# Gated retention block: totals of o's squares taken as rows by one product with a constant, and o scaled by a row in SBUF

## The chip, the core and the metric

The kernel runs on one core of a Trainium2 chip. The core has TensorE (PE, matrix products into PSUM), VectorE (DVE), ScalarE (ACT), GpSimd (POOL, which can't read PSUM) and the DMA queue of SyncE (SP). They run side by side and wait for each other by semaphores. The metric is the device time of one execution in microseconds. An f32 product stands as two records in the trace.

## What is computed

From the reference, cut to what matters. xn is the layer norm of x; T is 128 tokens, 8 chunks to each of 4 sequences, so 32 chunks.

```python
h = rmsnorm(xn, qkv_norm_w);  q, k, v = h @ quant(qkv_w).T
# per chunk of 128 tokens, 16 heads of 64:
o   = scale * (masked(q k^T) v  +  decay * q S);   S = lam_T * S + k_decayed^T v
out = o * rsqrt(mean(o*o) + 1e-6) * norm_w                     # first norm
out = out * rsqrt(mean(out*out) + 2**-23) * proj_norm_w        # second norm
s   = out @ quant(proj_w).T
g   = silu(xn @ ternary(ffn_w).T + bias)
result = x + s * g
```

Both norms of o together are one factor for each token, worked out from two totals over the 1024 channels: A = mean(o*o) and B = mean((o*norm_w)**2). The factor is (F32_EPS * (A + NORM_EPS) + B) ** -0.5.

## The kernel before

An iteration i takes two chunks, c = 0 and 1; there are NB = 16 iterations, and chunk number g = 2i + c. Channels lie on the partitions, so o of a chunk is 8 tiles of 128 channels by 128 tokens (ow, o_hi, o_lo). The order on each engine is written out by hand in tensor_program, vector_program, scalar_program and gpsimd_program, and nothing is moved by a scheduler.

The path of one chunk from its outputs to its projection:

- DVE weight_o (L1406) takes o out of PSUM with its channel weights into ow; ACT square_o makes the squares sq.
- POOL sum_squares (L2182, L2186, L2191) folds the squares over the 8 tiles into sq_sum[:, c], two planes of 128 channels by 128 tokens, one for A and one for B.
- PE output_scale (L857) multiplies each plane, as the stationary operand, by the column mean_w: two columns of totals, tokens on the partitions. For the three chunks of summed_at_once, (0,0), (1,0) and (15,1), it takes the totals from sq itself (L851) instead.
- DVE output_scale (L1429, L1431) makes F32_EPS * (A + NORM_EPS) + B, one column og.
- POOL output_scale (L2197) raises the column to the power -0.5, then (L2201) puts it on the diagonal diag of the identity.
- PE spread_gamma (L868) multiplies diag by the constant matrix mean_sq, which puts the factors as a row on all partitions, in PSUM.
- DVE scale_o (L1415) multiplies ow by that row; ACT high_o (L1898) and DVE split_o (L1422) split it into o_hi and o_lo.
- PE project_out (L880) waits for o_lo.

In the steady iterations (i >= 3) PE does the totals of chunk (i, 0) between the ffn products p7 and p3 (L680), its spread after p4, then the outputs of (i, 1) (L830, L834), update_state (L811), and both halves of project_out(i, 0). The totals of chunk (i, 1) come in the next iteration, between project_qk 1 and 2 (L747), the spread between 2 and 3, and project_out(i, 1) after project_qk 3 and k_product p1. On DVE low_b_sum (L1222) stands between output_scale and scale_o there, on chunk (i, 0) it is the gate work take_z12 and take_z21 (L1285).

Of the kernel before, what the change touches and what calls it, by code (L numbers as in the profile page):

```python
# [5 lines left out]
ALU = mybir.AluOpType  # L6
# [7 lines left out]
P = 128  # L14
BANK = 512
T = 128
CHUNKS = 2
# [19 lines left out]
def program(nc, x, qkv_w, proj_w, decay, ffn_w, ffn_b, norm_cols, x_turned, out):  # L37
# [17 lines left out]
    with ExitStack() as ctx:  # L55
# [92 lines left out]
        norm_pair = sb("norm_pair", [P, 2, CHUNKS, 2])  # L148
        og = sb("og", [P, 2, 4])
        diag = sb("diag", [P, CHUNKS, T])  # L150
        sum_cols = sb("sum_cols", [P, PR, 2])
# [309 lines left out]
        for i in range(BY_TOKENS):  # L461
            if i > 0:
                for j in range(PR):
                    ring_uses.append(("qk", i, j))
                    if j == 1:
                        ring_uses.append(("total", i - 1, 1))
                    if j == 2:
                        ring_uses.append(("spread", i - 1, 1))
                    if j in (4, 6):
                        ring_uses.append(("proj", i - 1, 1, j // 2 - 2))  # L470
                if i == 1:
                    ring_uses += [("v", 1, 0, 0), ("v", 1, 0, 1)]
                else:
                    ring_uses += [("v product", i, "p1"), ("v product", i, "p5"), ("v product", i, "p6")]
# [42 lines left out]

        def one_bank(i, c):

            return i > 1 and c == 0  # L520

        def bank_of(*use):
            if use[0] == "spread" and one_bank(*use[1:]):
                use = ("total", *use[1:])
            return ring_n[use] % NG

        def emptied(use):
# [26 lines left out]
            if kind == "k":  # L554
                return s_kl, HALF * passes_on(chunk(use[1], use[2])) + use[3] + 1
            if kind == "total" and not one_bank(*use[1:]):
                return s_gvar, 2 * chunk(use[1], use[2]) + 2
            if kind in ("total", "spread"):
                return s_os, chunk(use[1], use[2]) + 1
# [10 lines left out]
        def summed_at_once(g):  # L570

            return g in (chunk(0, 0), chunk(1, 0), chunk(NB - 1, 1))

        def sums(g):
# [22 lines left out]
        def tensor_program(pe):  # L597
# [166 lines left out]
            def scores(i, c):  # L764
# [10 lines left out]
                for half in range(HALF):  # L775
                    if g > 0 and half == 1:
                        pe.wait_ge(s_st, 2 * passes_on(g))
                        if c == 0 and aside(i - 1, 1):
                            pe.wait_ge(s_os, g)
                    for j in range(CPH):  # L780
# [59 lines left out]
            def output_scale(i, c):  # L840
# [14 lines left out]
                pe.wait_ge(s_red, sums(chunk(i, c)))  # L855
                for kind in range(2):
                    ins = pe.matmul(to[:, kind:kind + 1], sq_sum[:, c, kind, :], mean_w[:, :],  # L857
                                    start=True, stop=True)
                ins.then_inc(s_sqt, 1)

            def spread_gamma(i, c):

                pe.wait_ge(s_gamma, chunk(i, c) + 1)
                if aside(i, c):
                    pe.wait_ge(s_os, chunk(i, c))
                elif not one_bank(i, c):
                    free_bank("spread", i, c)
                pe.matmul(spread_of(i, c), mean_sq[:, :], diag[:, c, :], start=True, stop=True).then_inc(s_spread, 1)  # L868
# [29 lines left out]
            def attention_by_tokens(i, c):  # L898
# [6 lines left out]
                else:  # L905
# [4 lines left out]
                    product(i, "p4")  # L910
                    spread_gamma(i, 0)
                outputs(i, c, 0)
# [12 lines left out]
            def attention(i, c):  # L925
# [19 lines left out]
                if c == 1:  # L945
                    if i > 1:
                        spread_gamma(i, 0)
                    if i == 0:
# [48 lines left out]
            for i in range(BY_TOKENS):  # L997
                if i > 0:
                    for j in range(PR):
                        project_qk(i, j)  # L1000
                        if j == 1:
                            output_scale(i - 1, 1)
                        if j == 2:
                            spread_gamma(i - 1, 1)
                        if j in (4, 6):
# [9 lines left out]
            for i in range(BY_TOKENS, NB):  # L1015
# [3 lines left out]
                project_qk(i, 2)  # L1019
                spread_gamma(i - 1, 1)  # L1020
                project_qk(i, 3)
# [22 lines left out]
        def vector_program(dve):  # L1044
# [364 lines left out]
            def scale_o(i, c):  # L1409
                g = chunk(i, c)  # L1410
                dve.wait_ge(s_ow, HALF * (g + 1))
                dve.wait_ge(s_spread, g + 1)
                spread = spread_of(i, c).unsqueeze(1)
                for rs in o_parts(i, c):
# [9 lines left out]
            def output_scale(i, c):  # L1424
                g = chunk(i, c)
                k = og[:, c, :]
                bank = total_of(i, c)
                dve.wait_ge(s_sqt, g + 1)
                dve.tensor_scalar(k[:, 0:1], bank[:, 0:1], NORM_EPS, None, ALU.add).then_inc(s_gvar, 1)  # L1429
                dve.wait_ge(s_gvar, 2 * g + 1)  # L1430
# [120 lines left out]
            dve.memset(mean_sq[:, :], 1.0 / C).then_inc(s_ones, 1)  # L1551
            dve.memset(neg_magic[:, :], -MAGIC).then_inc(s_ones, 1)
            norm_stats(0, 0)
            norm_stats(0, 1)
# [516 lines left out]
        def gpsimd_program(pool):  # L2071
# [121 lines left out]
            def output_scale(i, c):  # L2193
                g = chunk(i, c)
                k = og[:, c, :]
                pool.wait_ge(s_gvar, 2 * g + 2)
                pool.tensor_tensor(k[:, 2:3], k[:, 1:2], halves[:, 3:4], ALU.pow).then_inc(s_gpow, 1)  # L2197
                pool.wait_ge(s_gpow, g + 1)
                if g >= CHUNKS:
                    pool.wait_ge(s_spread, g - CHUNKS + 1)  # L2200
                pool.tensor_scalar(diag[:, c, :], ident[:, :], k[:, 2:3], O_SCALE * C, ALU.mult, ALU.mult).then_inc(s_gamma, 1)  # L2201
# [235 lines left out]
```

## Time and profile before

| | |
|---|---|
| median of 3 runs | 1341.57 us (1341.17 to 1342.4) |
| the profiled execution | 1341.38 us, its span 1340.1 us |
| PE busy | 1312.0 us, 98% of the span |
| DVE, POOL, ACT busy | 934.7, 635.5, 583.5 us |

Busy is the time in which an engine has an instruction in work. Instructions on PE overlap, so what one costs is read from the distance of the starts before and after it. The idle time of an engine matters only where PE waits for it.

### The profile page before, as it was taken

Reading aid. Unit: us, or ns where it says so; the run is one execution under the profiler, and the core shown is the slowest. Engines: PE = TensorE matmul, PEld = TensorE weight load, DVE = VectorE, ACT = ScalarE, POOL = GpSimd, SP = SyncE. Lnnn points to the kernel's source line nnn. Section 1 sums busy time; section 2 is a strip of 40 time slices with the busy share of each in tenths; the row PEclk is TensorE's granted clock in tenths of the full one; section 3 lists DMA queues with packets and bytes.
Section 4 is the critical chain, followed back from the end, with each engine's and each line's share of the span. In section 5 each row is a group of like instructions: output and inputs, shape, how many; then the busy total and the mean of one; then the engine's idle time right before and its main releaser. Section 6 shows DMA issues by size and latency. Waiting matters only on the chain.

```text
span 1340.1 us, 25937 instructions
## 1 busy us (share of the span) xinstructions
PE 1312.0 (98%) x10409; PEld 842.5 (63%) x10409; DVE 934.7 (70%) x1489; ACT 583.5 (44%) x1139; POOL 635.5 (47%) x532
## 2 busy tenths in 40 slices
PE   4999999999999999999999999999999999999998
PEld 2577767674656657566675656657566575656655
DVE  7887467785666957667575776957667686776835
ACT  5884143343434544444353434544344453434521
POOL 1432877952544535447341654535435352654432
PEclk9999999999999999999999999999999999999999
DMA  9521111203021030300303021030301303020000
GB/s 363 234 95 64 72 33 38 97 17 119 2 71 64 17 118 1 121 15 17 118 17 118 2 96 40 17 119 1 127 9 21 114 17 119 1 88 17 33 32 32
DMA packets 33432, 90.32 MB, mean 67 GB/s; under 512 B 10529, under 2 KB 10785, under 8 KB 33314
## 3 DMA queue, kind: packets, MB, share of 16 engines
q1 hardware_dynamic: 33024, 88.65, 18.7%
q8 instruction: 83, 1.36, 0.4%
q14 instruction: 35, 0.29, 0.1%
q10 hardware_dynamic: 290, 0.02, 0.0%
HBM read 71.85 MB, written 16.81 MB: 66 GB/s over the span
## 4 chain that ended last, share of the span: by engine, by line
PE 89%; POOL 3%; DVE 3%; ACT 2%; issue 2%; DMA 1%; SPq 0%; POOLq 0%; ACTq 0%; DVEq 0%
PE ring L747 19%; PE ring L880 15%; PE ring L706 13%; PE ring L732 12%; PE ring L680 11%; PE att_ps L784 4%; PE att_ps L830 3%; PE att_ps L834 3%; PE ring L796 2%; PE att_ps L811 2%; PE ring L759 1%; POOL sq L2186 1%; PE ring L655 1%; DMA raw<-in_ffn_w 1%; ACT junk L1700 1%
## 5 line engine op out<-in xcount | busy, mean ns | idle before, releaser
L747 PE MATMUL ring<-b_lo,qkv_q 128*128 128x256 f16 x1216 | 268.2, 273 | 0.0
L747 PE MATMUL ring<-b_hi,qkv_q 128*128 128x256 f16 x1216 | 268.2, 272 | 0.0
L880 PE MATMUL ring<-proj_q,o_hi 128*128 128x512 fp8e4 x496 | 188.1, 379 | 3.0 <-DVE o_lo L1422 3.0
L880 PE MATMUL ring<-proj_q,o_lo 128*128 128x512 fp8e4 x496 | 188.0, 379 | 0.0
L2142 POOL TENSOR_TENSOR gate_even<-gate_even,bias 128x512 f32<-128x512 f32 x14 | 19.8, 1414 | 275.4 <-ACT gate_even L1819 275.4
L2182 POOL TENSOR_TENSOR sq<-sq,cols 128x1024 f32<-128x1024 f32 x29 | 55.1, 1900 | 165.5 <-DVE b_lo L1254 157.3
L747 PEld LDWEIGHTS ring<-b_hi,qkv_q 128*128 128x128 fp8e4 x1216 | 120.3, 99 | 15.6
L747 PEld LDWEIGHTS ring<-b_lo,qkv_q 128*128 128x128 fp8e4 x1216 | 118.9, 98 | 15.7
L2208 POOL TENSOR_TENSOR xt<-xt,gate_even 128x512 f32<-128x512 f32 x58 | 88.2, 1531 | 69.7 <-DVE gate_even L1442 68.5
L2186 POOL TENSOR_TENSOR sq<-sq 128x1024 f32<-128x1024 f32 (+1 forms) x58 | 109.5, 1888 | 4.5
L1843 ACT ACTIVATE gate_even<-gate_even 128x512 f32<-128x512 f32 x60 | 37.6, 629 | 154.7 <-DVE gate_even L1285 154.7
L834 PE MATMUL att_ps<-arena 128*64 128x128 f32 x1024 | 94.9, 273 | 0.0
L1859 ACT ACTIVATE arena<-ring,wscale 128x512 f32<-128x512 f32 x64 | 44.0, 687 | 116.0 <-PE ring L747 116.0
L1285 DVE SCALAR_TENSOR_TENSOR gate_even<-ring,ln,gate_even 128x512 f32<-128x512 f32 x70 | 52.5, 751 | 53.8 <-PE ring L680 53.8
L1351 DVE TENSOR_TENSOR arena<-att_ps,mask 128x512 f32<-128x512 f32 x128 | 79.4, 682 | 14.1 <-PE att_ps L784 14.1
L830 PE MATMUL att_ps<-arena 128*64 128x128 f32 x896 | 88.5, 276 | 0.0
L880 PEld LDWEIGHTS ring<-proj_q,o_hi 128*128 128x128 f16 x496 | 48.6, 98 | 60.9 <-DVE o_lo L1422 4.1
L880 PEld LDWEIGHTS ring<-proj_q,o_lo 128*128 128x128 f16 x496 | 48.5, 98 | 56.0
L2157 POOL TENSOR_TENSOR arena<-arena,lam_q 128x512 f32<-128x512 f32 x56 | 72.9, 1322 | 2.6 <-PE att_ps L834 2.6
L1804 ACT ACTIVATE gate_odd<-ring,wscale 128x512 f32<-128x512 f32 x26 | 17.9, 687 | 122.7 <-PE ring L732 122.7
L784 PEld LDWEIGHTS att_ps<-arena 64*128 64x128 f32 x1024 | 59.7, 188 | 13.8 <-issue 13.8
L1238 DVE SCALAR_TENSOR_TENSOR gate_odd<-ring,wscale,gate_odd 128x512 f32<-128x512 f32 x26 | 19.5, 750 | 68.2 <-PE ring L732 68.2
(257 smaller groups left out, 3249.1 us busy)
## 6 DMA issues: line engine op xcount, KB each, us to landing
xt<-in_x SPq DMA_DIRECT2D x62, 512.0 KB, 8.3
out<-xt SPq DMA_DIRECT2D x31, 512.0 KB, 3.1
raw<-in_qkv_w SPq DMA_DIRECT2D x24, 512.0 KB, 15.7
y<-in_x_turned SPq DMA_DIRECT2D x14, 512.0 KB, 6.8
y_odd<-in_x_turned SPq DMA_DIRECT2D x14, 512.0 KB, 7.7
raw<-in_ffn_w SPq DMA_DIRECT2D x8, 512.0 KB, 9.9
norm_rows<-norm_out SPq DMA_DIRECT2D x14, 256.0 KB, 6.0
raw<-in_proj_w SPq DMA_DIRECT2D x6, 512.0 KB, 4.5
```

Source lines behind the costliest of these rows:

```text
L680: ins = pe.matmul(ring[:, b, :], of[:, j, :], weights_of(weights)[:, j, :], start=(begins and j == 0 and k == 0), stop=(j == CPH - 1 and k ...
L706: ins = pe.matmul(ring[:, b, :], of[:, j, :], v_weights_of(weights)[:, j, :], start=(name in ("p1", "p5") and j == 0 and k == 0), stop=(j ...
L732: ins = pe.matmul(ring[:, b, :], of[:, j, :], k_weights_of(weights)[:, j, :], start=(name in ("p1", "p5") and j == 0 and k == 0), stop=(j ...
L747: ins = pe.matmul(ring[:, b, e * BT:(e + 1) * BT], qkv_q[:, cb, o:o + P], part[:, cb, :], start=(cb == 0 and part is b_hi), stop=(cb == NC ...
L784: ins = pe.matmul(att_ps[:, 2 * half + e, j, :], k_t[rows, r, ts], q_t[rows, r, ts], start=True, stop=True)
L830: pe.matmul(att_ps[e * D:(e + 1) * D, half, j, :], state[:, passes_on(g) % 2, r, e * D:(e + 1) * D], q_decay[:, r, :], start=True, stop=Fa ...
L834: ins = pe.matmul(att_ps[e * D:(e + 1) * D, half, j, :], v_tok[:, c, r * P + e * D:r * P + (e + 1) * D], scores_m[:, half, e, j, :], start ...
L880: ins = pe.matmul(ring[:, b, :], part[:, cb, :], proj_q[:, cb, cs], start=(cb == 0 and k == 0), stop=(cb == NCB - 1 and k == 1))
L1351: dve.tensor_tensor(scores_m[:, half, e, :, :], att_ps[:, 2 * half + e, :, :], mask[:, e, half * CPH:(half + 1) * CPH, :], ALU.mult).then_ ...
L2157: pool.tensor_tensor(q_decay[:, hs, :], q_t[:, hs, c * T:(c + 1) * T], lam_q[:, hs, :], ALU.mult).then_inc(s_ql, 1)
L2186: pool.tensor_tensor(sq[:, :, 0:m, :], sq[:, :, 0:m, :], sq[:, :, m:2 * m, :], ALU.add).then_inc(s_sqw, 1)
L2208: pool.tensor_tensor(o, o, gate_of(i)[:, c, cs], ALU.add).then_inc(s_add, 1)
```

## The change

For the 29 chunks outside summed_at_once the totals are taken the other way round: the constant matrix mean_o is the stationary operand, and the two planes of sq_sum stream through it as 256 columns. The result is both totals as rows, the same on all partitions. DVE adds them to one row of 128 tokens in SBUF (the row is the first plane of sq_sum, used anew), POOL raises the whole 128x128 tile to the power -0.5 into diag, and scale_o reads diag, in SBUF, without a further product. The constant factors O_SCALE and C that were put on with the diagonal go into mean_o and the eps. The three chunks of summed_at_once keep column, diagonal and spread.

```diff
+        mean_o = sb("mean_o", [P, P])
...
-                for kind in range(2):
-                    ins = pe.matmul(to[:, kind:kind + 1], sq_sum[:, c, kind, :], mean_w[:, :],
-                                    start=True, stop=True)
-                ins.then_inc(s_sqt, 1)
+                pe.wait_ge(s_ones, 7)
+
+                pe.matmul(to[:, 0:2 * T], mean_o[:, :], sq_sum[:, c, :, :].rearrange("p k t -> p (k t)"),
+                          start=True, stop=True).then_inc(s_sqt, 1)
...
-                    spread_gamma(i, 0)
...
-                spread_gamma(i - 1, 1)
...
                 dve.wait_ge(s_ow, HALF * (g + 1))
-                dve.wait_ge(s_spread, g + 1)
-                spread = spread_of(i, c).unsqueeze(1)
+                if summed_at_once(g):
+                    dve.wait_ge(s_spread, spreads(g))
+                    spread = spread_of(i, c).unsqueeze(1)
+                else:
+                    dve.wait_ge(s_gamma, g + 1)
+                    spread = diag[:, c, :].unsqueeze(1)
...
+                if not summed_at_once(g):
+
+                    row = sq_sum[:, c, 0, :]
+                    dve.tensor_scalar(row, bank[:, 0:T], NORM_EPS / O_SCALE ** 2, F32_EPS, ALU.add,
+                                      ALU.mult).then_inc(s_gvar, 1)
+                    dve.wait_ge(s_gvar, 2 * g + 1)
+                    dve.tensor_tensor(row, row, bank[:, T:2 * T], ALU.add).then_inc(s_gvar, 1)
+                    return
...
+            dve.memset(mean_o[:, :], 1.0 / C / O_SCALE ** 2).then_inc(s_ones, 1)
...
                 pool.wait_ge(s_gvar, 2 * g + 2)
+                if not summed_at_once(g):
+                    pool.tensor_tensor(diag[:, c, :], sq_sum[:, c, 0, :], halves[:, 3:4].to_broadcast([P, T]),
+                                       ALU.pow).then_inc(s_gamma, 1)
+                    return
```

The rest of the diff follows from this: the bank of the totals is free when DVE has added them (s_gvar) and no longer when o is scaled (s_os), the ring of PSUM banks loses the uses of the spread, and the counts of the three spreads that are left are renumbered.

PE in iteration 5, around the end of the ffn products and the outputs (L830 and L834 before are L829 and L833 after, L680 is L679). Before:

```order
L680 MATMUL ring<-ffn_sum,a_hi 128x512
L680 MATMUL ring<-ffn_sum,a_lo 128x512
L868 MATMUL att_ps<-diag,mean_sq 128x128
L830 MATMUL att_ps<-arena 64x128 x2
L834 MATMUL att_ps<-arena 64x128 x2
```

After:

```order
L679 MATMUL ring<-ffn_sum,a_hi 128x512
L679 MATMUL ring<-ffn_sum,a_lo 128x512
L829 MATMUL att_ps<-arena 64x128 x2
L833 MATMUL att_ps<-arena 64x128 x2
L829 MATMUL att_ps<-arena 64x128 x2
```

The spread is gone, and the outputs follow the products at once. POOL in iteration 5, from the last fold of chunk (5, 0) to the add of the output after the totals of (5, 1) (sq and sq_sum are the folds, og and diag the scale, arena the decay of the state, xt the output). Before:

```order
L2191 TENSOR_TENSOR sq_sum<-sq 128x256
L2169 TENSOR_TENSOR arena<-arena,lam_T 64x8x64 x2
L2197 TENSOR_TENSOR og<-og,halves 128x1
L2201 TENSOR_SCALAR diag<-ident,og 128x128
L2182 TENSOR_TENSOR sq<-sq,cols 128x1024
L2186 TENSOR_TENSOR sq<-sq 128x2x512
L2186 TENSOR_TENSOR sq<-sq 128x2x256
L2191 TENSOR_TENSOR sq_sum<-sq 128x256
L2197 TENSOR_TENSOR og<-og,halves 128x1
L2201 TENSOR_SCALAR diag<-ident,og 128x128
L2208 TENSOR_TENSOR xt<-xt,gate_even 128x512 x2
```

After:

```order
L2194 TENSOR_TENSOR sq_sum<-sq 128x256
L2172 TENSOR_TENSOR arena<-arena,lam_T 64x8x64 x2
L2201 TENSOR_TENSOR diag<-sq_sum,halves 128x128
L2185 TENSOR_TENSOR sq<-sq,cols 128x1024
L2189 TENSOR_TENSOR sq<-sq 128x2x512
L2189 TENSOR_TENSOR sq<-sq 128x2x256
L2194 TENSOR_TENSOR sq_sum<-sq 128x256
L2201 TENSOR_TENSOR diag<-sq_sum,halves 128x128
L2215 TENSOR_TENSOR xt<-xt,gate_even 128x512 x2
```

The power on one column and the diagonal (two instructions) are one power on 128 columns now, at the same places. DVE in iteration 5, from its totals of chunk (5, 0) to o_lo. Before:

```order
L1429 TENSOR_SCALAR og<-att_ps 128x1
L1431 SCALAR_TENSOR_TENSOR og<-og,att_ps 128x1
L1285 SCALAR_TENSOR_TENSOR gate_even<-ring,ln,gate_even 128x512 x2
L1415 TENSOR_TENSOR ow<-ow,att_ps 128x1024
L1254 SCALAR_TENSOR_TENSOR b_lo<-y,cols,b_hi 128x128 x4
L1422 TENSOR_TENSOR o_lo<-ow,o_hi 128x1024
```

After:

```order
L1426 TENSOR_SCALAR sq_sum<-att_ps 128x128
L1429 TENSOR_TENSOR sq_sum<-sq_sum,att_ps 128x128
L1275 SCALAR_TENSOR_TENSOR gate_even<-ring,ln,gate_even 128x512 x2
L1409 TENSOR_TENSOR ow<-ow,diag 128x1024
L1244 SCALAR_TENSOR_TENSOR b_lo<-y,cols,b_hi 128x128 x4
L1416 TENSOR_TENSOR o_lo<-ow,o_hi 128x1024
```

Nothing moved here; two instructions are wider, and the factor of scale_o is read from SBUF.

## Rows read from the trace of the kernel before

**Rows 1.** The page: busy time and share of the span; PE and its clock in 40 slices.

```profile
PE 1312.0 (98%) x10409; PEld 842.5 (63%) x10409; DVE 934.7 (70%) x1489; ACT 583.5 (44%) x1139; POOL 635.5 (47%) x532
...
PE   4999999999999999999999999999999999999998
...
PEclk9999999999999999999999999999999999999999
```

**Rows 2.** The waits of PE: line, releaser, us in total, times, longest.

```profile
PE ring L880 <- DVE o_lo L1422: 3.0, 5, 1.0
```

**Rows 3.** Timeline of PE around totals and spread: start us, us, instruction.

```profile
291.40 0.27 PE L747 MATMUL ring<-b_lo,qkv_q 128*128 128x256 f16 x1
291.50 0.50 PE L857 MATMUL att_ps<-mean_w,sq_sum 128*128 128x1 f32 x4
291.87 0.27 PE L747 MATMUL ring<-b_hi,qkv_q 128*128 128x256 f16 x1
...
295.25 0.27 PE L747 MATMUL ring<-b_lo,qkv_q 128*128 128x256 f16 x1
295.36 0.39 PE L868 MATMUL att_ps<-diag,mean_sq 128*128 128x128 f32 x2
295.58 0.27 PE L747 MATMUL ring<-b_hi,qkv_q 128*128 128x256 f16 x1
```

**Rows 4.** Instructions by line: count, ns minimum, median, maximum, first and last start.

```profile
L2197 POOL TENSOR_TENSOR og<-og,halves x32: 550/570/960, 113.7 to 1326.3; 128x1 f32<-128x1 f32 x32
...
L2081 POOL TENSOR_TENSOR ln<-ln x32: 188/190/651, 9.1 to 1186.0; 128x1 f32<-128x1 f32 x32
...
L2191 POOL TENSOR_TENSOR sq_sum<-sq x29: 723/728/1060, 128.7 to 1310.4; 128x256 f32<-128x256 f32 x29
...
L1119 DVE TENSOR_SCALAR sq_sum<-sq_sum x1: 220/220/220, 36.5 to 36.5; 128x128 f32<-128x128 f32 x1
```

**Rows 5.** Timeline of POOL: the power on three columns, early and in the steady part.

```profile
7.96 0.87 POOL L2078 TENSOR_TENSOR ln<-ln,halves 128x3 f32<-128x3 f32 x1 [5.95 <-DVE ln L1142]
...
457.62 1.37 POOL L2078 TENSOR_TENSOR ln<-ln,halves 128x3 f32<-128x3 f32 x1
```

**Rows 6.** Timelines of POOL, DVE and PE, chunk (5, 0), from the power to project_out.

```profile
510.68 0.58 POOL L2197 TENSOR_TENSOR og<-og,halves 128x1 f32<-128x1 f32 x1 [0.17 <-DVE og L1431]
...
513.34 0.75 DVE L1285 SCALAR_TENSOR_TENSOR gate_even<-ring,ln,gate_even 128x512 f32<-128x512 f32 x1 [0.98 <-PE ring L680]
514.01 1.21 DVE L1415 TENSOR_TENSOR ow<-ow,att_ps 128x1024 f32<-128x1024 f32 x1
...
516.40 1.23 DVE L1422 TENSOR_TENSOR o_lo<-ow,o_hi 128x1024 f16<-128x1024 f32 x1
...
518.03 0.39 PE L880 MATMUL ring<-proj_q,o_hi 128*128 128x512 fp8e4 x1
```

**Rows 7.** The same of chunk (5, 1), in iteration 6.

```profile
532.91 0.56 POOL L2197 TENSOR_TENSOR og<-og,halves 128x1 f32<-128x1 f32 x1 [2.01 <-DVE og L1431]
...
536.96 1.21 DVE L1415 TENSOR_TENSOR ow<-ow,att_ps 128x1024 f32<-128x1024 f32 x1
...
539.51 1.22 DVE L1422 TENSOR_TENSOR o_lo<-ow,o_hi 128x1024 f16<-128x1024 f32 x1
...
541.24 0.38 PE L880 MATMUL ring<-proj_q,o_hi 128*128 128x512 fp8e4 x1
```

**Rows 8.** Timeline of PE at the start: after its first idle stretch, and then.

```profile
11.59 1.97 PE L636 MATMUL ring<-ident,y 128*128 128x128 f32 x8 [11.59 <-DVE y L1154]
...
26.16 0.58 PE L655 MATMUL ring<-ffn_q,a_hi 128*128 128x512 fp8e4 x1
...
29.52 0.57 PE L655 MATMUL ring<-ffn_q,a_hi 128*128 128x512 fp8e4 x1
...
30.15 0.38 PE L655 MATMUL ring<-ffn_q,a_hi 128*128 128x512 fp8e4 x1
...
38.13 0.38 PE L655 MATMUL ring<-ffn_q,a_lo 128*128 128x512 fp8e4 x1
```

More of the change, by code:

```diff
@@ L466, in program @@
                         ring_uses.append(("total", i - 1, 1))
-                    if j == 2:
-                        ring_uses.append(("spread", i - 1, 1))
                     if j in (4, 6):
@@ L516, in spread_of @@
             return att_bank(3)[:, P:P + T] if aside(i, c) else ring[:, bank_of("spread", i, c), 0:T]
-        def one_bank(i, c):
-            return i > 1 and c == 0
         def bank_of(*use):
-            if use[0] == "spread" and one_bank(*use[1:]):
-                use = ("total", *use[1:])
             return ring_n[use] % NG
@@ L555, in emptied @@
                 return s_kl, HALF * passes_on(chunk(use[1], use[2])) + use[3] + 1
-            if kind == "total" and not one_bank(*use[1:]):
+            if kind == "total":
                 return s_gvar, 2 * chunk(use[1], use[2]) + 2
-            if kind in ("total", "spread"):
+            if kind == "spread":
                 return s_os, chunk(use[1], use[2]) + 1
@@ L572, in summed_at_once, with spreads @@
             return g in (chunk(0, 0), chunk(1, 0), chunk(NB - 1, 1))
+        def spreads(g):
+            return sum(summed_at_once(k) for k in range(g + 1))
         def sums(g):
@@ L778, in scores @@
                         if c == 0 and aside(i - 1, 1):
-                            pe.wait_ge(s_os, g)
+                            pe.wait_ge(s_gvar, 2 * g)
                     for j in range(CPH):
@@ L855, in output_scale @@
                 pe.wait_ge(s_red, sums(chunk(i, c)))
-                for kind in range(2):
-                    ins = pe.matmul(to[:, kind:kind + 1], sq_sum[:, c, kind, :], mean_w[:, :],
-                                    start=True, stop=True)
-                ins.then_inc(s_sqt, 1)
+                pe.wait_ge(s_ones, 7)
+                pe.matmul(to[:, 0:2 * T], mean_o[:, :], sq_sum[:, c, :, :].rearrange("p k t -> p (k t)"),
+                          start=True, stop=True).then_inc(s_sqt, 1)
             def spread_gamma(i, c):
                 pe.wait_ge(s_gamma, chunk(i, c) + 1)
-                if aside(i, c):
-                    pe.wait_ge(s_os, chunk(i, c))
-                elif not one_bank(i, c):
+                if not aside(i, c):
                     free_bank("spread", i, c)
@@ L945, in attention @@
                 if c == 1:
-                    if i > 1:
-                        spread_gamma(i, 0)
                     if i == 0:
@@ L1002, in tensor_program @@
                             output_scale(i - 1, 1)
-                        if j == 2:
-                            spread_gamma(i - 1, 1)
                         if j in (4, 6):
@@ L1019, in tensor_program @@
                 project_qk(i, 2)
-                spread_gamma(i - 1, 1)
                 project_qk(i, 3)
@@ L2196, in output_scale @@
                 pool.wait_ge(s_gvar, 2 * g + 2)
+                if not summed_at_once(g):
+                    pool.tensor_tensor(diag[:, c, :], sq_sum[:, c, 0, :], halves[:, 3:4].to_broadcast([P, T]),
+                                       ALU.pow).then_inc(s_gamma, 1)
+                    return
                 pool.tensor_tensor(k[:, 2:3], k[:, 1:2], halves[:, 3:4], ALU.pow).then_inc(s_gpow, 1)
-                pool.wait_ge(s_gpow, g + 1)
-                if g >= CHUNKS:
-                    pool.wait_ge(s_spread, g - CHUNKS + 1)
+                pool.wait_ge(s_gpow, spreads(g))
+                if c == 0 and i > 0:
+                    pool.wait_ge(s_spread, spreads(g) - 1)
                 pool.tensor_scalar(diag[:, c, :], ident[:, :], k[:, 2:3], O_SCALE * C, ALU.mult, ALU.mult).then_inc(s_gamma, 1)
```

## The prediction

> **What bounds the kernel now.** I read the page first: the busy shares, then who waits for whom on PE, then the timeline of single instructions around the two operations that the diff touches, and at last the rows of POOL. TensorE is busy for 1312.0 of 1340.1 us, DVE for 70% and POOL for 47% [rows 1]. Its slices read 9 from the second to the last but one [rows 1], so nearly all of its idle time lies in the start. From the first projection on PE waits almost never; the largest wait of the steady part is for DVE's o_lo ahead of project_out, 3.0 us in five places [rows 2]. So two things count: PE time that goes, and a chain beside PE that becomes longer than its cover. The profiled execution took 1341.38 us, its span 1340.1 us, the median of the three timed runs is 1341.57 us. The sum is made on 1341.4.
>
> **What the change does, PE first.** There are 32 chunks; three of them, (0,0), (1,0) and (15,1), keep the old way (summed_at_once). For the other 29, of each chunk:
>
> Removed: the two products with one column. They stand as four records (each f32 product has two). The last L747 before them starts at 291.40, the next after them at 291.87, 0.47 us, where neighbours stand 0.11 us apart: they cost 0.36 us [rows 3].
>
> Removed: the spread of the diagonal. Between 295.25 and 295.58 lie 0.33 us; less 0.11 it costs 0.22 us for 128 columns, 0.11 us for each of its two records [rows 3].
>
> Added: one f32 product with 256 columns. No row has just this. By the spread's columns it is twice 0.22, 0.44 us, with the weights loaded under the work before, as the spread's are. If its weight loads stood in the open, the four loads inside the 0.36 us are the nearest row, 0.09 us each, so 0.18 more; the low end is 0.36, what the old pair takes. I take 0.44 because the spread has the same type and the same stationary size.
>
> PE saves 0.36 + 0.22 - 0.44 = 0.14 us a chunk, 29 * 0.14 = 4.1 us (with the bounds, from 6 us gained to 1 us lost).
>
> **DVE.** The two tiny operations (L1429, L1431) become two on 128x128. A 128x128 tensor_scalar took 0.22 us [rows 4]; two are 0.44 us, which puts off POOL's power by 0.44 us if the tiny ones had been free. They had a start-up each too, so I take 0.2 us, and 0.3 where the longer product ends later as well. scale_o has the same form and 1024 elements; its second operand now comes from SBUF. o_lo, which reads two SBUF operands of the same size, takes 1.23 us against its 1.21 us [rows 6], so I take no change. It no longer waits for PE's spread.
>
> **POOL, the step on which all hangs.** Before, POOL raised one column to the power -1/2 (0.57 us, 32 times) and spread it on the diagonal. After, it does one power on 128x128, and DVE's scale_o, ACT's high_o, DVE's split_o and PE's project_out stand behind it. No row shows a power on 128 columns. The rows show it on one column, 0.55 to 0.57 us, and on three, 0.87 us, where a plain one-column tensor_tensor takes 0.19 us [rows 4, 5]. So a column more costs (0.87 - 0.57) / 2 = 0.15 us, and 128 columns cost 0.57 + 127 * 0.15 = 19.6 us, if every column goes through the same code in turn. (The three-column power of 1.37 us in the steady part stands beside DVE work; in the stall below DVE is idle, so I don't extrapolate from it.) The other bound is that the price of the columns vanishes: a plain tensor_tensor takes 0.73 us for 256 columns [rows 4], 2.1 ns a column, so 0.57 + 0.27 = 0.8 us. Between 0.8 and 19.6 us I take the high end, since the two rows of the power itself lie on it: from one to three columns it grew seventy times as fast as the plain operation does.
>
> The Trainium skill ("GPSIMD Engine Reference", section 3.1) gives every two-input elementwise operation of this engine some 2.6 cycles an element at 1.2 GHz, without an exception for the power. The plain rows agree (2.1 ns a column); the power's rows do not (150 ns). By the page the new power would be the 0.8 us of the low bound, and the sum that of the first rival.
>
> **What of 19.6 us is hidden.** Chunk (5,0): the old power starts at 510.68; the new one at 510.9, and ends at 530.5. scale_o started at 514.01, held there by the gate work of L1285 that ends at 514.09; o_lo ended at 517.63 and project_out started at 518.03 [rows 6]. scale_o comes 16.5 us later, less the 0.35 us that o_lo had to spare (0.40, and 0.05 to hand it over): PE stands still for 16.2 us, with nothing queued that it may do (project_out is next in order, and project_qk behind it). There are 14 such chunks. Chunk (5,1): the old power starts at 532.91, the new one at 533.2, to 552.8; scale_o started at 536.96, o_lo ended at 540.73 and project_out started at 541.24 [rows 7]. That is 15.9 less 0.45, 15.5 us, 15 times (the first of them has a longer cover; some 2 us in all, left out). On DVE weight_o, add_state, the b_lo parts and the sums of y queue behind scale_o, on ACT qk_out(i, 3) and the squares behind high_o, on POOL add_out and norm_scale; they all move with PE, which has stopped too, so they add nothing that I can show. 14 * 16.2 + 15 * 15.5 = 226.8 + 232.5 = 459 us.
>
> **The clock after a stall.** After PE's first idle stretch of 11.6 us, with little work behind it, the f16 products of 512 columns start 0.42 us apart (26.16 to 29.52, eight steps), which is 1.2 GHz, and later 0.216 us (30.15 to 38.13, 37 steps), 2.4 GHz, although the granted clock of the page reads full speed there [rows 1, 8]. Eight steps at half speed lose 8 * 0.2 = 1.6 us. A stall of 16 us is longer than that idle stretch, so I charge 1.6 us for each of 29, 47 us; the bounds are nothing and twice that.
>
> **The sum.** 1341.4 - 4.1 + 459 + 47 = 1843 us. With the smallest and the largest undisturbed power on one column, 0.55 and 0.58 us [rows 4, 6], a column is 0.16 or 0.145 us and the power 20.9 or 19.0 us, which moves the sum by +38 or -17 us, and the clock by -47 to +47: the forecast's own range is 1780 to 1930.
>
> **Rivals.**
> First, faster: the power works through many columns much faster than through three, at 0.8 to 3.2 us. The point from which it decides is the cover: from 510.9 to 514.0 in (5,0), 3.1 us plus 0.35; 3.7 plus 0.45 in (5,1) [rows 6, 7]. Below some 3.4 us all is hidden, and only PE's saving is left: 1341.4 - 4.1 = 1337.3 us. For it: POOL is idle for half of the time, one and three columns tell little of a long loop, and the plain operation runs at 2.1 ns a column. Against it: the 0.15 us for each of the second and third column.
> Second, between: a column costs 0.035 to 0.12 us, the power 5 to 15 us. Each of 29 stalls is P less some 3.9: at 8 us 29 * 4.1 = 119 us, and up to 47 for the clock: some 1456 to 1503, 1370 to 1710 over the case.
> Third, no change: the power is hidden, but the product shows its weight loads (0.18 us, 29 times, 5 us), or the cover of (i,0) is lost. PE now reaches project_out the spread's 0.22 us earlier there, and o_lo had 0.35 us to spare. 1339 to 1344 us.
> That the power isn't on the path at all is excluded by the program: scale_o waits for it.
>
> **How the numbers follow.** The forecast 0.46, faster 0.30, between 0.18, no change 0.06. The likeliest is the forecast, 1843. Faster and no change together are more than 2 in 10, so the range must reach down to them: from 1334 (PE's saving at its bound, with the five small waits for o_lo partly gone) up to 1880, which leaves out the dearest fifth or so of the forecast's own range. About 0.2% of the time, 2.7 us, is what a measurement of this kernel can tell from no change. Faster 0.30, same 0.06, slower 0.46 + 0.18 = 0.64.
>
> **What would show it.** In the profile after, POOL's tensor_tensor on diag: 19 to 21 us each for the forecast, under 3.4 for the faster rival. PE's waits: project_out for DVE's o_lo, some 29 times 16 us, and PE's busy share down to about 70%; or no such wait. The product on PE: 0.44 us between its neighbours. DVE's scale_o should wait for POOL's diag, and the first products after each wait should stand 0.42 us apart. The forecast is wrong if POOL's power on 128 columns isn't near twenty microseconds; all else in it is small.

## The result, and the profile after

The changed kernel takes 1931.58 us (median of six runs, 1929.78 to 1932.68), the kernel before beside it 1341.58 us. The ratio is 1.4396, with a 95% interval of 1.4377 to 1.4414. That is 590 us more, where the forecast said 502 more (1843); it lies above the range's end of 1880 too.

The page of the changed kernel, its busy times, slices and chain. Beside [rows 1] PE falls from 98% to 71% and POOL, 47% before, stands at 62%; PE's slices show pits of 6, and its granted clock, full throughout before, moves between 7 and 9.

```profile
span 1928.3 us, 25619 instructions
...
PE 1371.1 (71%) x10293; PEld 845.5 (44%) x10293; DVE 947.3 (49%) x1490; ACT 583.2 (30%) x1139; POOL 1198.0 (62%) x503
...
PE   6996966695666966669666696666966669666595
...
PEclk9998987798787987879878797787977879778797
...
POOL diag L2201 30%; PE ring L705 9%; PE ring L876 7%; PE ring L731 7%; PE ring L679 5%; POOL sq L2189 3%; PE att_ps L783 3%; DVE ow L1409 2%; DVE b_lo L1244 2%; PE ring L746 2%; DVE o_lo L1416 2%; POOL sq L2185 2%; DVE a_lo L1183 1%; PE ring L795 1%; PE att_ps L829 1%
...
L2201 POOL TENSOR_TENSOR diag<-sq_sum,halves 128x128 f32<-128x128 f32 x29 | 601.9, 20754 | 86.9 <-DVE sq_sum L1429 86.6
```

One power takes 20.75 us (mean ns in the last row), 29 times, and stands on the path with 30% of the span. The wait for it runs through three engines: DVE's scale_o waits for POOL, PE's project_out (L876) waits for DVE's o_lo. The waits of PE (line, releaser, us in total, times, longest); [rows 2] had 3.0 us in five places here.

```profile
PE ring L876 <- DVE o_lo L1416: 532.2, 30, 19.1
```

Chunk (4, 0), to be laid beside (5, 0) in [rows 6]. POOL, DVE and PE of the changed kernel: start, us, instruction, idle time before it.

```profile
550.13 20.76 POOL L2201 TENSOR_TENSOR diag<-sq_sum,halves 128x128 f32<-128x128 f32 x1
...
570.99 1.23 DVE L1409 TENSOR_TENSOR ow<-ow,diag 128x1024 f32<-128x1024 f32 x1 [18.04 <-POOL diag L2201]
...
573.40 1.23 DVE L1416 TENSOR_TENSOR o_lo<-ow,o_hi 128x1024 f16<-128x1024 f32 x1
...
574.68 0.61 PE L876 MATMUL ring<-proj_q,o_hi 128*128 128x512 fp8e4 x1 [17.94 <-DVE o_lo L1416]
575.08 0.63 PE L876 MATMUL ring<-proj_q,o_lo 128*128 128x512 fp8e4 x1
575.51 0.64 PE L876 MATMUL ring<-proj_q,o_hi 128*128 128x512 fp8e4 x1
```

PE stands still for 17.9 us, and the products after it stand 0.43 us apart and no longer 0.216. Granted clock of PE in three stretches behind this stall (window, its us, PE busy, clock, share of DMA, GB/s):

```profile
574.60:577.00 2.40, 2.32 (x6) 0.50 0.00 0
577.00:580.00 3.00, 3.00 (x8) 0.50 0.00 0
...
582.00:590.00 8.00, 8.00 (x64) 1.00 0.00 0
```

Chunk (4, 1), to be laid beside (5, 1) in [rows 7]: the timelines of POOL and DVE.

```profile
592.79 20.73 POOL L2201 TENSOR_TENSOR diag<-sq_sum,halves 128x128 f32<-128x128 f32 x1 [5.58 <-DVE sq_sum L1429]
613.49 3.47 POOL L2215 TENSOR_TENSOR xt<-xt,gate_even 128x512 f32<-128x512 f32 x2
...
592.90 2.64 DVE L1212 TENSOR_TENSOR b_sum_lo<-arena,b_sum_hi 128x512 f16<-128x512 f32 x4 [0.19 <-ACT b_sum_hi L1769]
613.62 2.21 DVE L1409 TENSOR_TENSOR ow<-ow,diag 128x1024 f32<-128x1024 f32 x1 [18.08 <-POOL diag L2201]
615.75 1.75 DVE L1183 TENSOR_TENSOR a_lo<-y_odd,a_hi 128x512 f16<-128x512 f32 x1
```

Here is something that the prediction had not seen. POOL's add_out (L2215) starts with the end of the power, at the same moment as scale_o, and scale_o takes 2.21 us instead of the 1.23 of chunk (4, 0); a_lo behind it takes 1.75 instead of 0.68. Before, scale_o of (5, 1) also ran beside add_out, but its factor then came from PSUM, and it took 1.21 us [rows 7]. POOL and DVE of the kernel before, just ahead of it:

```profile
534.91 3.26 POOL L2208 TENSOR_TENSOR xt<-xt,gate_even 128x512 f32<-128x512 f32 x2
...
533.38 3.66 DVE L1222 TENSOR_TENSOR b_sum_lo<-arena,b_sum_hi 128x512 f16<-128x512 f32 x4 [0.55 <-ACT b_sum_hi L1766]
```

There the four low_b_sum, which have two SBUF inputs, took 3.66 us. The power itself does not do this: in the changed kernel low_b_sum (L1212) runs beside it in 2.64 us for four.

Two things came as said. The product with 256 columns starts at 591.46 and its next neighbour at 591.89, 0.43 us where 0.44 was taken. And POOL's power, DVE's wait for it and PE's wait for o_lo stand where the forecast put them.

### The profile page after: what moved, and what is told of

It is laid out like the page before. It is cut to its first block, busy times and chain, and to the rows that moved or that the text cites. A ratio compares the mean times of both kernels' runs of the same rounds, so it can differ in the third digit from the quotient of the medians.

```text
span 1928.3 us, 25619 instructions
## 1 busy us (share of the span) xinstructions
PE 1371.1 (71%) x10293; PEld 845.5 (44%) x10293; DVE 947.3 (49%) x1490; ACT 583.2 (30%) x1139; POOL 1198.0 (62%) x503
## 4 chain that ended last, share of the span: by engine, by line
POOL 39%; PE 38%; DVE 11%; issue 8%; ACT 2%; DMA 1%; SPq 0%; DVEq 0%; POOLq 0%; ACTq 0%
POOL diag L2201 30%; PE ring L705 9%; PE ring L876 7%; PE ring L731 7%; PE ring L679 5%; POOL sq L2189 3%; PE att_ps L783 3%; DVE ow L1409 2%; DVE b_lo L1244 2%; PE ring L746 2%; DVE o_lo L1416 2%; POOL sq L2185 2%; DVE a_lo L1183 1%; PE ring L795 1%; PE att_ps L829 1%
## 5 line engine op out<-in xcount | busy, mean ns | idle before, releaser
L2201 POOL TENSOR_TENSOR diag<-sq_sum,halves 128x128 f32<-128x128 f32 x29 | 601.9, 20754 | 86.9 <-DVE sq_sum L1429 86.6
L876 PE MATMUL ring<-proj_q,o_hi 128*128 128x512 fp8e4 x496 | 226.0, 456 | 532.2 <-DVE o_lo L1416 532.2
L876 PEld LDWEIGHTS ring<-proj_q,o_hi 128*128 128x128 f16 x496 | 56.5, 114 | 619.7 <-DVE o_lo L1416 541.6
L1409 DVE TENSOR_TENSOR ow<-ow,diag 128x1024 f32<-128x1024 f32 x29 | 50.3, 1735 | 524.4 <-POOL diag L2201 524.4
L876 PE MATMUL ring<-proj_q,o_lo 128*128 128x512 fp8e4 x496 | 222.8, 449 | 0.0
L1901 ACT ACTIVATE o_hi<-ow 128x1024 f16<-128x1024 f32 x31 | 32.8, 1057 | 559.9 <-DVE ow L1409 559.9
L2215 POOL TENSOR_TENSOR xt<-xt,gate_even 128x512 f32<-128x512 f32 x58 | 92.4, 1604 | 90.0 <-DVE gate_even L1444 89.9
L833 PE MATMUL att_ps<-arena 128*64 128x128 f32 x1024 | 94.9, 273 | 0.0
L876 PEld LDWEIGHTS ring<-proj_q,o_lo 128*128 128x128 f16 x496 | 55.9, 113 | 75.7 <-issue 37.3
L829 PE MATMUL att_ps<-arena 128*64 128x128 f32 x896 | 88.5, 276 | 0.0
L1444 DVE SCALAR_TENSOR_TENSOR gate_even<-ring,wscale,gate_even 128x512 f32<-128x512 f32 x58 | 43.4, 748 | 77.3 <-PE ring L876 77.1
## 6 DMA issues: line engine op xcount, KB each, us to landing
raw<-in_qkv_w SPq DMA_DIRECT2D x24, 512.0 KB, 15.6
```

The costliest lines, as they stand in the source:

```text
L829: pe.matmul(att_ps[e * D:(e + 1) * D, half, j, :], state[:, passes_on(g) % 2, r, e * D:(e + 1) * D], q_decay[:, r, :], start=True, stop=Fa ...
L833: ins = pe.matmul(att_ps[e * D:(e + 1) * D, half, j, :], v_tok[:, c, r * P + e * D:r * P + (e + 1) * D], scores_m[:, half, e, j, :], start ...
L876: ins = pe.matmul(ring[:, b, :], part[:, cb, :], proj_q[:, cb, cs], start=(cb == 0 and k == 0), stop=(cb == NCB - 1 and k == 1))
L1409: dve.tensor_tensor(ow[:, rs, :], ow[:, rs, :], spread.to_broadcast([P, rs.stop - rs.start, T]), ALU.mult).then_inc(s_os, 1)
L2201: pool.tensor_tensor(diag[:, c, :], sq_sum[:, c, 0, :], halves[:, 3:4].to_broadcast([P, T]), ALU.pow).then_inc(s_gamma, 1)
L2215: pool.tensor_tensor(o, o, gate_of(i)[:, c, cs], ALU.add).then_inc(s_add, 1)
```

## The experiments

### Without the power

The power becomes a product of the same shape; all else stays.

```diff
-                                       ALU.pow).then_inc(s_gamma, 1)
+                                       ALU.mult).then_inc(s_gamma, 1)
```

> The changed kernel with the power on 128x128 replaced by a multiplication of the same shape on the same engine (the power is left out, so o's factor isn't the reference's). Theory A, the length of the power is all that makes the changed kernel slower: POOL's step takes some 0.45 us and is hidden, PE keeps its 0.14 us a chunk, 1337 us (1334 to 1339.5), no wait of project_out for o_lo above 1 us. Rival B, other parts of the change cost as well (two wide DVE operations, scale_o reading SBUF, the product with 256 columns): some of the 590 us stay, at the least 1344 us.

Measured: 1350.46 us, ratio 1.0064 (1.0050 to 1.0078). So of the 590 us the power carries 581. But the number is not A's 1337: without its power the changed kernel is still slower than the kernel before, by 8.6 us. The waits of PE show eighteen small ones for o_lo:

```profile
PE ring L876 <- DVE o_lo L1416: 14.1, 18, 1.0
```

Thirteen of them, 10.2 us, are in chunks (i, 1), where the kernel before has none; the other five stand where its five were. POOL and DVE of this kernel in chunk (5, 1):

```profile
535.67 0.40 POOL L2201 TENSOR_TENSOR diag<-sq_sum,halves 128x128 f32<-128x128 f32 x1 [2.16 <-DVE sq_sum L1429]
536.03 3.39 POOL L2215 TENSOR_TENSOR xt<-xt,gate_even 128x512 f32<-128x512 f32 x2
...
535.78 4.78 DVE L1212 TENSOR_TENSOR b_sum_lo<-arena,b_sum_hi 128x512 f16<-128x512 f32 x4 [0.19 <-ACT b_sum_hi L1769]
540.49 1.21 DVE L1409 TENSOR_TENSOR ow<-ow,diag 128x1024 f32<-128x1024 f32 x1
```

A short POOL step lets add_out start early, beside DVE's four low_b_sum. They take 4.78 us; beside the power they took 2.64. scale_o waits behind them. This is B's number with another cause, and it became a question of its own, below.

### POOL held back in the changed kernel

To test the contention, POOL begins add_out of a chunk c=1 only when o_lo of that chunk is there.

```diff
+                    if c == 1:
+                        pool.wait_ge(s_olo, g + 1)
```

> The changed kernel, in which POOL, after the power of chunk (i,1), waits for that chunk's o_lo before it goes on to add_out; nothing else is changed. Theory A, scale_o of chunk (i,1) takes 2.2 us (1.2 in chunk (i,0)) because POOL's add_out runs beside it: it falls to 1.22 us, the a_lo behind it from 1.75 to 0.7 us, each of 15 stalls becomes 2 us shorter, 1931 - 30 = 1900 us. Rival B, the long form belongs to the operand in SBUF, or the time is taken elsewhere: scale_o stays at 2.2 us and the time at 1930 us or above (POOL's work then comes later).

Measured: 1904.83 us (1904.08 to 1906.81), ratio 1.4199, 26.8 us less than the changed kernel. scale_o on all 29 chunks (count, ns minimum, median, maximum), in this kernel:

```profile
L1409 DVE TENSOR_TENSOR ow<-ow,diag x29: 1224/1225/1226, 155.7 to 1877.1; 128x1024 f32<-128x1024 f32 x29
```

and in the changed kernel:

```profile
L1409 DVE TENSOR_TENSOR ow<-ow,diag x29: 1224/2209/2212, 156.4 to 1902.2; 128x1024 f32<-128x1024 f32 x29
```

The long form is gone, and PE's mean stall on c=1 falls from 18.65 to 16.64 us (15 stalls); on c=0 it stays at 17.96 (14 stalls). The contention is shown. It is 30 us of PE's waits and some 27 us of time: the wait on POOL has a price of its own, 3.4 us for which PE now waits for the diagonal of an old-way chunk. The Trainium skill ("SBUF — State Buffer", section "Who interferes with whom") says that a DVE instruction with two SBUF inputs contends with a GpSimd instruction that reads SBUF, and that one with at most one SBUF input, outside the two-port modes, doesn't. These rows agree: 1.21 us with the factor in PSUM, 2.21 with it in SBUF, both beside add_out. The power is an exception that the rule does not have: it reads SBUF too, and low_b_sum takes 2.64 us for four beside it, as it does with POOL idle (in the last version without the power, below).

### PE kept at work in the stall

Products that nobody reads, 39 or 42 of 256 columns, ahead of project_out in 26 of the stalls.

```diff
+                if half == 0 and chunk(i, c) > chunk(BY_TOKENS - 1, 0):
+                    pe.wait_ge(s_gvar, 2 * chunk(i, c) + 2)
+                    for _ in range(42 if c else 39):
+                        pe.matmul(att_bank(3)[:, 2 * T:4 * T], mean_sq[:, :],
+                                  mask[:, 0, 0:2, :].rearrange("p r t -> p (r t)"), start=True, stop=True)
```

> The changed kernel with PE kept at work in the stall: ahead of project_out(i, c, 0), from chunk (2,1) to (15,0), 42 (c=1) or 39 (c=0) f32 products of 256 columns into columns that nobody reads, some 18 and 17 us at full speed, so that they end about 1 us before o_lo. Theory A, PE runs at 1.2 GHz for 5 to 6 us after each stall because it stood idle, which costs 2.9 us (c=0) and 2.4 us (c=1): 13 * 2.9 + 13 * 2.4 = 69 us come back, 1862 us, granted clock 1.0 in the steady part, L876 back at 379 ns. Rival B, the slow first products have another cause (operands, waits for weights) or the clock doesn't follow the idle time: 1925 us or more.

Measured: 1876.66 us (1875.30 to 1877.31), ratio 1.3985, mean granted clock 0.985 where it was 0.855. It is 54.9 us less, while the way from POOL's power to project_out keeps its length (3.8 to 4.2 us on c=0, 6.0 to 6.4 on c=1): the price of the half-speed stretch after a stall is shown, at 54.9 / 26 = 2.1 us for each. The expectation, 1862 us, was too low, since it had read 2.65 us for each from two stalls, (4, 0) and (4, 1). By the granted clock in the changed kernel's trace PE is busy at half speed for 2.6 to 5.9 us after each of the 29 stalls, 122 us together, and half of that, 61 us, is lost.

### Both at once

> The changed kernel with both mends at once: add_out of c=1 behind o_lo, and PE kept at work with products that nobody reads during 26 of the stalls. If contention (27 us) and clock (55 us) are separate terms they add up: 1850 us (1843 to 1858), and what is left over 1337 us is the power's own stall, 14 times 17.9 and 15 times 17.1 us. If they are one effect, the time stays above 1868.

The products are 38 instead of 42 on c=1, where the stall is shorter now. Measured: 1849.85 us (1848.81 to 1851.76), ratio 1.3794. 1931.58 - 26.8 - 54.9 = 1849.9: the two terms are separate and add up.

### The power alone, in ten widths

The kernel before, with powers and products of several widths in a row at the end of POOL's program.

```diff
+            for n in (1, 2, 3, 4, 8, 16, 32, 64, 128, 256):
+                pool.tensor_tensor(dst[:, at:at + n], src[:, 0:n], halves[:, 3:4].to_broadcast([P, n]),
+                                   ALU.pow).then_inc(s_widths, 1)
```

> The kernel before, with powers on 1, 2, 3, 4, 8, 16, 32, 64, 128 and 256 columns of 128 partitions, multiplications on 1, 3, 16 and 128 columns, and a power on 128 columns of 16 partitions at the end of POOL's program, where POOL is idle and the end of the kernel waits for nothing else; its total time doesn't matter. Theory A, each column goes through the same code in turn: 0.57 + 0.158 * (n - 1) us, so 1.67 at 8, 5.5 at 32, 10.5 at 64, 20.6 at 128, 40.9 at 256; 16 partitions take as long as 128. Rival B, a start-up or a slower path weighs at small widths and the price bends: 64 columns above 12 us or below 9.

Measured (POOL's instructions by shape: busy us, mean ns; L2301 is the power, L2305 the product, L2308 the power on 16 partitions):

```profile
L2301 POOL TENSOR_TENSOR sq<-lam_q,halves 128x128 f32<-128x128 f32 x1 | 20.7, 20722 | 0.0
L2308 POOL TENSOR_TENSOR sq<-lam_q,halves 16x128 f32<-16x128 f32 x1 | 20.7, 20707 | 0.0
L2301 POOL TENSOR_TENSOR sq<-lam_q,halves 128x64 f32<-128x64 f32 x1 | 10.5, 10517 | 0.0
L2301 POOL TENSOR_TENSOR sq<-lam_q,halves 128x32 f32<-128x32 f32 x1 | 5.4, 5411 | 0.0
...
L2301 POOL TENSOR_TENSOR sq<-lam_q,halves 128x4 f32<-128x4 f32 x1 | 1.4, 1431 | 0.0
L2301 POOL TENSOR_TENSOR sq<-lam_q,halves 128x3 f32<-128x3 f32 x1 | 0.9, 856 | 0.0
...
L2301 POOL TENSOR_TENSOR sq<-lam_q,halves 128x1 f32<-128x1 f32 x1 | 0.6, 550 | 0.0
L2305 POOL TENSOR_TENSOR sq<-lam_q,halves 128x128 f32<-128x128 f32 x1 | 0.4, 397 | 0.0
```

From one to three columns a column costs (0.856 - 0.550) / 2 = 0.153 us, the forecast's slope. From 32 to 128 columns it costs (20.722 - 5.411) / 96 = 0.159 us, but the fourth alone costs 0.58 us. From 32 columns on the length is nearly in proportion to the columns, and 16 partitions take as long as 128. A product of the same shape takes 0.397 us.

### A quarter of the power

The power on 32 columns, a product on the other 96.

```diff
-                    pool.tensor_tensor(diag[:, c, :], sq_sum[:, c, 0, :], halves[:, 3:4].to_broadcast([P, T]),
-                                       ALU.pow).then_inc(s_gamma, 1)
+                    n = 32
+                    pool.tensor_tensor(diag[:, c, n:T], sq_sum[:, c, 0, n:T], halves[:, 3:4].to_broadcast([P, T - n]),
+                                       ALU.mult).then_inc(s_gpart, 1)
+                    pool.wait_ge(s_gpart, g + 1 - spreads(g))
+                    pool.tensor_tensor(diag[:, c, 0:n], sq_sum[:, c, 0, 0:n], halves[:, 3:4].to_broadcast([P, n]),
+                                       ALU.pow).then_inc(s_gamma, 1)
```

> The changed kernel with the power on 32 columns of the row only and a product on the other 96 (so it leaves out three quarters of the power): POOL's step is 0.40 + 5.41 us, 14.9 us less than after. Theory (the stall follows the power one for one once the cover is used up): PE waits 17.9 - 14.9 = 3.0 us in each c=0 and 19.2 - 14.9 = 4.3 us in each c=1, 106 us in all, 1444 us, and 1500 if PE runs at half speed after these short waits too. Rival (part of a power of 20.7 us is a fixed price, or the cover is larger than 3.4 us): under 1400.

Measured: 1498.91 us (1497.82 to 1500.93), ratio 1.1175. PE's waits:

```profile
PE ring L877 <- DVE o_lo L1417: 105.2, 30, 4.6
```

105 us of waits where 106 were expected: beyond its cover the stall follows the power one for one, and no part of the 20.75 us is a fixed price. The clock is the rest of the time: by the granted clock in this trace PE is busy at half speed for 116 us, of which 58 us are lost. So stalls of 3 to 5 us bring it down too.

### Why 1350 and not 1337 without the power

First, the version without the power, with POOL held back as above.

> Leaves out the power (a product of the same shape stands in its place, as in the run with the product before) and lets POOL begin add_out of a chunk c=1 only when DVE's o_lo of that chunk is there. Theory A: the 8.6 us that the product version lost came from POOL's add_out (3.39 us) running beside DVE's low_b_sum; with add_out behind o_lo the four low_b_sum take about 3 us instead of 4.78, PE's waits for o_lo (14.1 us) fall under 2, and the time is PE's saving alone, 1337 us (1335.5 to 1339). Rival B: the longer product on PE, the two wide rows on DVE or scale_o reading SBUF lengthen the chain: the time stays at 1347 or more.

Measured: 1353.79 us (1350.42 to 1354.15), ratio 1.0082. At first sight A has fallen. The waits of PE in this kernel:

```profile
PE ring L705 <- DVE arena L1220: 6.6, 1, 6.6
PE ring L876 <- DVE o_lo L1416: 4.0, 5, 1.0
PE ring L864 <- POOL diag L2210: 3.4, 1, 3.4
```

The eighteen waits for o_lo are five again, as before the change, but two new ones stand there, once each, for 10 us together. They follow the first two chunks c=1, where POOL's sums of the weights and the power of the old-way chunk (1, 0) are queued behind the new wait. After the second PE runs at half speed for 6.8 us, another 3.4 us lost.

The same wait in the kernel before the change:

> The kernel before with the same wait on POOL alone (add_out of c=1 behind o_lo). If add_out beside DVE's work is what cost it its five waits for o_lo (3.0 us), the time falls to 1338.5 (1337.5 to 1340.5). If POOL becomes late with norm_scale instead, the time rises, to 1344 or more.

Measured: 1356.54 us (1356.04 to 1356.96), ratio 1.0110. All of it is lost in the first three iterations: at project_out of (2, 0) the kernel is 15.6 us behind the kernel before, at that of (15, 0) 15.5. In the steady part the wait gains nothing there, so the expected 3 us were wrong: the five waits for o_lo stay (3.1 us in five places). They are all on c=0, in (1, 0), (3, 0), (7, 0), (11, 0) and (15, 0), which a wait on c=1 does not touch; their cause was not looked for.

Then the wait only from iteration 2 on.

```diff
-                    if c == 1:
+                    if c == 1 and i > 1:
                         pool.wait_ge(s_olo, g + 1)
```

> Leaves out the power (a product of the same shape stands in its place). As the product version with add_out of c=1 behind o_lo, but only for chunks (i,1) with i of 2 and more: the two chunks before lost 5.4 and 8 us once there, since POOL's sums of the weights wait behind. Theory A: without these two losses only PE's saving is left, 0.15 us a chunk: 1337.5 us (1336 to 1339.5). Rival B: part of the 8.6 us of the product version has another cause and stays: 1342 or more.

Measured: 1337.34 us (1336.99 to 1338.39), ratio 0.9970 (0.9959 to 0.9982). POOL and DVE of chunk (5, 1), to be laid beside those of the version without the wait:

```profile
538.15 2.49 POOL L2217 TENSOR_TENSOR xt<-xt,gate_even 128x512 f32<-128x512 f32 x2 [6.48 <-DVE o_lo L1416]
...
531.38 2.64 DVE L1212 TENSOR_TENSOR b_sum_lo<-arena,b_sum_hi 128x512 f16<-128x512 f32 x4 [0.19 <-ACT b_sum_hi L1769]
533.95 1.21 DVE L1409 TENSOR_TENSOR ow<-ow,diag 128x1024 f32<-128x1024 f32 x1
```

low_b_sum is back at 2.64 us. So A holds: with add_out away from low_b_sum the loss is gone. It was 1350.46 - 1337.34 = 13.1 us and not 8.6, since PE's saving had hidden a part of it; 10.2 us of it are PE's waits for o_lo (14.1 us against 3.9), and where the rest lies was not followed. The change without its power is worth 1341.6 - 1337.3 = 4.3 us, 0.15 us a chunk; the wait by itself gained nothing in the steady part of the kernel before.

### A version that beats both

What PE gained came from fewer products. There is a way to get this without a wide power: mean(s) and mean(s w^2) meet as mean(s (w^2 + eps)) + 1e-6 eps, with s the squares, so one weighted plane and one column are enough. From the kernel before:

```diff
+                dve.tensor_scalar(cols[:, 1, :], cols[:, 1, :], F32_EPS, None, ALU.add).then_inc(s_cols_made, 1)
...
-                for kind in range(2):
-                    ins = pe.matmul(to[:, kind:kind + 1], sq_sum[:, c, kind, :], mean_w[:, :],
-                                    start=True, stop=True)
-                ins.then_inc(s_sqt, 1)
+                pe.matmul(to[:, 0:1], sq_sum[:, c, 1, :], mean_w[:, :], start=True, stop=True).then_inc(s_sqt, 1)
...
+                dve.tensor_scalar(k[:, 1:2], bank[:, 0:1], NORM_EPS * F32_EPS, None, ALU.add).then_inc(s_gvar, 2)
```

> A version meant to beat both: of before, with one plane of squares instead of two. The two sums of a token, mean(s) and mean(s w^2), meet as mean(s w^2) + eps (mean(s) + 1e-6) = mean(s (w^2 + eps)) + 1e-6 eps, so one weighted sum is enough: one product with one column instead of two on PE (0.18 us less in each of 29 chunks), one tiny operation of DVE instead of two, POOL's folds on half the elements. Theory: 5.2 us less, 1336.4 us; since DVE's saved operation lets POOL begin add_out some 0.2 us earlier, up to 3 us of it may be lost on c=1 as in the product version: 1335.5 to 1339.5. Rival: PE's one-column products hide each other's weight loads, and nothing is gained, 1341.

Measured: 1343.94 us (1342.94 to 1344.67), ratio 1.0017 (1.0008 to 1.0026): slower, outside what was expected. Eighteen waits for o_lo (13.1 us) stand there, by the same mechanism: one DVE operation less ahead of POOL's power, and add_out begins early enough to run into low_b_sum (mean 1.22 us for one, 0.97 before). With POOL held back, first everywhere:

> The one-plane version with add_out of c=1 behind o_lo as well. Theory: both gains add up, 1334 us (1332 to 1337), with PE's waits for o_lo under 1 us. Rival: the wait on POOL costs more than it gives: above the one-plane version without it.

Measured: 1346.89 us, ratio 1.0041 (1.0028 to 1.0053): the rival came true, with the same loss in the first iterations. Then from iteration 2 on:

> The version meant to beat both: one plane of squares, and add_out of c=1 behind o_lo only for i of 2 and more. From chunk (4,0) to the end the earlier version of it gained 5.9 us on the kernel before, 0.25 us a chunk; without the losses at the start the time should be 1335 us (1333.5 to 1337.5). Rival: something else at the start is lost too: 1340 or more.

Measured: 1331.34 us (1330.68 to 1331.80), ratio 0.9923 (0.9911 to 0.9936), below the 1333.5 us at which the expectation ended. It beats the kernel before by 10.3 us and the changed one by 600. Its waits for o_lo are as before, five with 3.0 us:

```profile
PE ring L877 <- DVE o_lo L1421: 3.0, 5, 1.0
```

Against the kernel before, the start of project_out moves forward by 0.45 us in most iterations, 0.22 us a chunk, and by 1.0 us more in the three where PE had waited for POOL's sq_sum at the totals (2.3 us in three places before, none now: the folds have half the elements). This is more than the 5.2 us first expected of one plane; about 1 us of the difference lies at the start of the execution and may belong to it alone.

## Why the prediction was wrong, point by point

**Direction and mechanism held.** The power is on the path, PE stands still 29 times for the time that it has no cover for, and runs at half speed after each stall. The rival "faster" falls by its own sign: the power takes 20.75 us, not under 3.4. "Between" and "no change" fall with it, and so does the price of 0.8 us by the Trainium skill ("GPSIMD Engine Reference", section 3.1) that the prediction weighed against its rows.

**The failed step is the sizing of the stall and of what follows it.** PE's waits came to 532.2 us where 459 were charged, the clock to 29 times 2.1, some 61 us, where 47 were. The PE saving (4.1 forecast, 4.3 measured without the power) was right. The terms make 532.2 - 3.0 + 61 - 4.3 = 586 us of the 590 measured. The 88 us between forecast and result divide as follows, but for 1 us.

- **The power**, 20.75 us instead of 19.6: 29 * 1.15 = 33 us. The slope was taken from one and three columns; the step at four columns and the slightly steeper long run lie beyond them. The text had 20.9 us as its bound.
- **POOL's add_out**: with the rest of the work behind the stall it was said to "add nothing that I can show", and that was wrong. It adds 2.0 us to each of 15 stalls on c=1, some 30 us of PE's waits. And "its second operand now comes from SBUF … I take no change" was wrong for the same reason. The o_lo row that stood for it ran with nothing on POOL that hurt it, so it could not show it. The rows for a warning were there: POOL's add_out begins directly behind the power, scale_o waits for just that, and low_b_sum of the kernel before took 3.66 us for four beside POOL's work, where one takes 0.68 at the least.
- **The cover**: some 10 us, nearly all on c=0. The forecast read it in (5, 0) alone, 518.03 - 510.9 = 7.13 us, and took it for all fourteen. In (5, 0) itself it held: the changed kernel has 7.01 us there, from the power's start to the stall's, and PE stands still for 17.54 us, where 16.2 and the 1.15 of the power make 17.35.

```profile
672.57 20.75 POOL L2201 TENSOR_TENSOR diag<-sq_sum,halves 128x128 f32<-128x128 f32 x1 [0.44 <-DVE sq_sum L1429]
...
697.12 0.61 PE L876 MATMUL ring<-proj_q,o_hi 128*128 128x512 fp8e4 x1 [17.54 <-DVE o_lo L1416]
```

But (4, 0), (8, 0) and (12, 0) have a cover of 6.61 us, and (2, 0), (3, 0), (7, 0), (11, 0) and (15, 0) one of 6.14. The trace of before has the same order, from the power's start to project_out: 7.35 us in (5, 0), 6.74 in (4, 0), and 6.55 in (3, 0) up to PE's wait. So 8.6 us are lost on c=0; 1.0 us is the wait of (1, 0), which stood there before.

- **The clock**: 2.1 us instead of 1.6 a stall, 14 us in all. The eight slow steps at the start of the kernel were the nearest row, and too short by a quarter. The bound of twice that held it.

**The range** ended at 1880, inside the forecast's own upper part, since the chance of "faster" had to be taken in below. But the forecast's own range, 1780 to 1930, with the dearest power and twice the clock, ends below the result too: all four errors went the same way, and the contention was in no bound at all.

**The rivals' prices.** "Faster" was priced at 1337.3. The held version without the power gives 1337.34 (1336.99 to 1338.39), so the sum for PE was right. But a power that vanished in this program would have given 1350.5: a POOL step shorter than the old one frees add_out to run into low_b_sum, which the rival's text did not have. "Between" was priced at 29 times (P - 3.9); with P = 5.8 that is 55 us, and 105 were measured, mostly because it left out the contention, some 30 us, and the shorter covers on c=0, some 9.

## What to carry to other kernels

Before a per-token value is spread to save a step, ask in which layout the dearest operation of its chain sees it: POOL's power costs 0.16 us for each column, on 16 partitions as on 128, so one column of 128 tokens takes 0.55 us and one row of them 20.7. When an operand moves from PSUM to SBUF, look at what the other engines do beside its reader at that moment, not at a row of the same shape elsewhere. And making one engine's step shorter moves its next step too: place that one on purpose, with a wait if need be, as the last version does.

## What the runs showed of the hardware that was not expected

A DVE tensor_tensor with both inputs in SBUF takes 2.21 us instead of 1.22 beside POOL's add, while beside POOL's power the same kind of work keeps its time (2.64 us for four low_b_sum).

After each of the 29 stalls of 16 to 19 us PE is at half speed from its first product. After the stalls of 2.7 to 4.0 us on c=0 in the version with a quarter of the power it is at half speed from the first product four times; ten times it begins at full speed and falls 0.7 to 1.3 us later. The length of the stall alone does not decide it: stalls of 2.65 and of 3.52 us are found on both sides. The timeline of PE after (5, 0) there:

```profile
566.62 0.39 PE L877 MATMUL ring<-proj_q,o_hi 128*128 128x512 fp8e4 x1 [2.66 <-DVE o_lo L1417]
566.85 0.38 PE L877 MATMUL ring<-proj_q,o_lo 128*128 128x512 fp8e4 x1
...
567.50 0.38 PE L877 MATMUL ring<-proj_q,o_hi 128*128 128x512 fp8e4 x1
567.71 0.56 PE L877 MATMUL ring<-proj_q,o_lo 128*128 128x512 fp8e4 x1
568.06 0.63 PE L877 MATMUL ring<-proj_q,o_hi 128*128 128x512 fp8e4 x1
568.49 0.63 PE L877 MATMUL ring<-proj_q,o_lo 128*128 128x512 fp8e4 x1
...
571.34 0.38 PE L877 MATMUL ring<-proj_q,o_hi 128*128 128x512 fp8e4 x1
571.56 0.38 PE L877 MATMUL ring<-proj_q,o_lo 128*128 128x512 fp8e4 x1
```

The products stand 0.216 us apart up to 567.71 and 0.43 from 568.06 to 571.05: a busy PE, at half speed for 3.3 us, for a stall that was already over.
